# A recommendation tower on one core: the first two blocks of embeddings put in rows by TensorE instead of through memory, and layer 1's weights asked for at another time

## The reference

```python
e = stack([tbl_f[ids[:, f]] for f in range(39)], axis=1)        # 512 x 39 x 16
def cin(X0, Xi, W, b):                                          # W: 128 x (39 * fields of Xi)
    return einsum('hjk,bjd,bkd->bhd', W.reshape(H, 39, -1), X0, Xi) + b[None, :, None]
X1 = cin(e, e, W0, b0)          # 39 x 39 products
X2 = cin(e, X1, W1, b1)         # 39 x 128
X3 = cin(e, X2, W2, b2)
z = concatenate([X1.sum(2), X2.sum(2), X3.sum(2)], axis=1)      # 512 x 384
h = relu(concatenate([z, dense_ctx], 1) @ W_top1 + b_top1)
h = relu(h @ W_top2 + b_top2)
y = h @ W_top3
```

## Time and profile before

| | us |
|---|---|
| median of 3 runs | 669.59 |
| lowest and highest | 668.69, 670.15 |
| the profiled execution's own time | 670.7 |
| its span in the trace | 668.9 |
| TensorE busy | 644.9 (96%) |
| GpSimd busy | 497.0 (74%) |
| ScalarE busy | 480.0 (72%) |
| VectorE busy | 458.9 (69%) |

### The profile page before, as it was taken

One profiled execution on the slowest core, in us unless ns is written; L12 is line 12 of the kernel. 1 busy time (PEld: TensorE's weight loads), 2 busy tenths in 40 slices (PEclk: granted clock), 3 DMA queues, 4 the chain that ended last, 5 costly groups with the idle time before them and its releaser, 6 DMA issues.

```text
span 668.9 us, 11234 instructions
## 1 busy us (share of the span) xinstructions
PE 644.9 (96%) x2676; PEld 479.0 (72%) x2676; DVE 458.9 (69%) x1183; ACT 480.0 (72%) x1737; POOL 497.0 (74%) x467
## 2 busy tenths in 40 slices
PE   3599999999999999999999999999999999999998
PEld 1387677777777777777787777777776777779773
DVE  1367777778686968777725786868687877774920
ACT  1457678878787879697815787878796978784912
POOL 5779888979797988888835797979888886553710
PEclk9989999999999999999999999999999999999999
DMA  6643515151514233251500514132241404002000
GB/s 159 140 100 80 124 26 118 36 120 13 128 27 102 54 75 79 44 111 34 119 11 2 119 13 108 25 81 51 46 85 28 103 10 118 4 4 93 2 0 1
DMA packets 68264, 43.32 MB, mean 65 GB/s; under 512 B 49483, under 2 KB 61710, under 8 KB 66458
## 3 DMA queue, kind: packets, MB, share of 16 engines
q1 hardware_dynamic: 56870, 38.04, 25.4%
q0 software_dynamic: 5184, 1.29, 2.3%
q10 hardware_dynamic: 6158, 3.45, 2.0%
HBM read 39.58 MB, written 1.96 MB: 62 GB/s over the span
## 4 chain that ended last, share of the span: by engine, by line
PE 94%; issue 2%; DVE 1%; DMA 1%; ACT 1%; ACTq 0%; POOLq 0%; POOL 0%; DVEq 0%
PE a_ps L704 40%; PE d_ps L704 25%; PE quad_ps L655 14%; PE quad_ps L758 5%; PE g_ps L745 5%; PE g_ps L814 1%; DMA g_sb<-w_dram 1%; PE quad_ps L672 1%; PE a_ps L871 1%; PE quad_ps L659 1%; PE d_ps L842 1%; ACT parts L930 0%; DVE parts L551 0%; DVE x2t L563 0%; PE a_ps L842 0%
## 5 line engine op out<-in xcount | busy, mean ns | idle before, releaser
L930 ACT ACTIVATE parts<-a_ps,xt 128x128 f32<-128x128 f32 x1536 | 424.1, 383 | 129.7 <-PE a_ps L704 115.3
L551 DVE SCALAR_TENSOR_TENSOR parts<-d_ps,xt,parts 128x128 f32<-128x128 f32 x704 | 201.7, 343 | 108.9 <-PE d_ps L704 98.9
L311 POOL TENSOR_TENSOR parts<-parts 128x512 f32<-128x512 f32 x128 | 163.5, 1293 | 99.3 <-ACT parts L930 98.0
L704 PE MATMUL a_ps<-w_hi,x_hi 128*128 128x512 f32 x384 | 181.3, 472 | 1.5 <-issue 1.5
L311 POOL TENSOR_TENSOR left<-parts 128x512 f32<-128x512 f32 x128 | 167.3, 1323 | 7.5 <-ACT parts L930 5.9
L285 POOL DMA_INDIRECT emb<-tables_dram,rows_now x150 | 144.0, 960 | 25.3 <-issue 18.5
L704 PE MATMUL a_ps<-w_hi,x_lo 128*128 128x512 f32 x384 | 152.4, 397 | 0.6 <-issue 0.6
L704 PE MATMUL a_ps<-w_lo,x_hi 128*128 128x512 f32 x384 | 151.4, 394 | 0.0
L704 PE MATMUL d_ps<-w_hi,x_hi 128*128 128x512 f32 (+1 forms) x256 | 127.0, 496 | 0.9 <-DVE parts L551 0.9
L655 PE MATMUL quad_ps<-products,w_sb 117*128 117x512 f32 (+1 forms) x210 | 107.4, 592 | 0.0
L704 PE MATMUL d_ps<-w_lo,x_hi 128*128 128x512 f32 (+1 forms) x256 | 97.8, 382 | 0.6 <-ACT xt L908 0.6
(11 more groups left out here) (72 smaller groups left out, 428.4 us busy)
## 6 DMA issues: line engine op xcount, KB each, us to landing
shifted<-x_rows SPq DMA_DIRECT2D x45, 312.0 KB
shifted<-x_rows SPq DMA_DIRECT2D x45, 234.0 KB
diag<-xt SPq DMA_DIRECT2D x240, 4.9 KB
rows<-x_rows SPq DMA_DIRECT2D x45, 78.0 KB
emb<-tables_dram,rows_now POOLq DMA_INDIRECT x150
w_sb<-w_dram SPq DMA_DIRECT2D x6, 384.0 KB
shifted<-x_first SPq DMA_DIRECT2D x12, 136.5 KB
g_sb<-w_dram ACTq DMA_DIRECT2D x2, 768.0 KB
```

What stands on the lines that cost most here:

```text
L311: nc.gpsimd.tensor_tensor(to, parts[:, i % 2, now:now + GF, :], parts[:, i % 2, more:more + GF, :], ALU.add).then_inc(pool_added, 1)
L551: nc.vector.scalar_tensor_tensor(now, d_ps[d % D_RING][:, H * at:H * (at + 1)], xt[:, u, i, j:j + 1], before, ALU.mult, ALU.add).then_inc( ...
L704: return nc.tensor.matmul(bank[:, 0:H * len(fields)], x[:, u, 128 * i:128 * (i + 1)], w[:, fields[0]:fields[-1] + 1, :].rearrange("p j h - ...
L930: last = nc.scalar.activation(parts[:, i % 2, 2 + GF * a + at, :], a_ps[(NA * i + a) % A_RING][:, H * at:H * (at + 1)], ACT.Copy, scale=xt ...
```

## The change

Blocks 0 and 1 of the first chunk no longer go through memory. Their gathered rows stand as (8 samples, 16 fields) by 16 elements over the partitions. VectorE spreads each row to eight copies of which all but its own sample's are zero (`spread_first`, a product with a table of ones, `spots`). TensorE sums this with a table of ones (`picker`) into the 39 fields as rows, three times over (`sum_rows`, three float32 matmuls); ScalarE copies this to `rows3` (`copy_first`); TensorE multiplies it with seven tables of ones (`turns`), which gives the seven rotated tiles in PSUM (`turn_rows`, seven float32 matmuls of 39 rows and 128 columns); and VectorE multiplies these with `rows3` (`multiply_turned`). The PSUM banks used are free at that time. `turn_rows(1)` stands behind group 0 of block 0.

The tables come with the small inputs on SP's queue: `masks` is 128 rows of 1468 bytes in place of `mask` (128 of 32 bytes), `turns` is 39 rows of 3276 bytes in place of `ident` (39 of 156 bytes). SP writes and loads only blocks 2 and 3. ScalarE issues the second and the third part of layer 1's weights together, once block 0's gathers have landed; before, the second part was issued at the start and the third after block 0's loads had landed. In VectorE's list `diag_first(0)` now stands ahead of block 1's products and of `split_w1(2)`.

```diff
+TURNED = 2
+TURN_AT = (0, 0)
+        turned_rows = [rows_ps[0:PK, 0:128], g_ps[0:PK, 0:128]]
+        turned_tiles = [(a_ps[0][0:PK, :], a_ps[1][0:PK, 128:512]), (g_ps[0:PK, :], quad_ps[0:PK, 128:512])]
 # SP
-            sp.dma_start(ident[:, :], ident_in).then_inc(small_loaded, 16)
-            sp.dma_start(mask[:, :], mask_in).then_inc(small_loaded, 16)
+            sp.dma_start(masks[:, :], mask_in).then_inc(small_loaded, 16)
+            sp.dma_start(turns[:, :, :], turns_in).then_inc(small_loaded, 16)
-            for i in range(BLKS):
+            for i in range(TURNED, BLKS):
                 write_first(i)
                 load_first(i)
 # VectorE
+            def spread_first(i):
+                dve.wait_ge(first_gathered[i], 16 * GATHERS0)
+                for g0, g1, parts in ((0, GATHERS0 - 1, 128), (GATHERS0 - 1, GATHERS0, LAST_G0)):
...
+                    last = nc.vector.tensor_tensor(to, rows, at, ALU.mult)
+                last.then_inc(spread_ready, 1)
+            def multiply_turned(i):
+                cols = slice(128 * i, 128 * (i + 1))
+                for half, (t0, t1) in enumerate(((0, FIRST_TILES), (FIRST_TILES, QT))):
+                    dve.wait_ge(turned, 2 * i + half + 1)
...
+                    last = nc.vector.tensor_tensor(products[0:PK, t0:t1, cols], tiles, rows, ALU.mult)
+                last.then_inc(first_products, 1)
...
+            spread_first(0)
             split_w1(0)
-            multiply_first(0)
+            multiply_turned(0)
             split_w1(1)
+            spread_first(1)
             low_first(0)
-            multiply_first(1)
+            diag_first(0)
+            multiply_turned(1)
             split_w1(2)
-            diag_first(0)
             first_body()
 # TensorE
+            def sum_rows(i):
+                pe.wait_ge(spread_ready, i + 1)
+                for g in range(GATHERS0):
+                    parts = 128 if g < GATHERS0 - 1 else LAST_G0
+                    mm = nc.tensor.matmul(turned_rows[i], picker[0:parts, g, :], spread[0:parts, i, g, :],
+                                          start=(g == 0), stop=(g == GATHERS0 - 1))
+                mm.then_inc(rows_turned, 1)
+            def turn_rows(i):
+                pe.wait_ge(first_rows, i + 1)
+                for half, (t0, t1) in enumerate(((0, FIRST_TILES), (FIRST_TILES, QT))):
+                    for t in range(t0, t1):
+                        mm = nc.tensor.matmul(turned_tiles[i][half][:, 128 * (t - t0):128 * (t - t0 + 1)], turns[:, t, :],
+                                              rows3[0:FIELDS, 128 * i:128 * (i + 1)], start=True, stop=True)
+                    mm.then_inc(turned, 1)
...
             pe.wait_ge(small_loaded, 64)
+            sum_rows(0)
+            turn_rows(0)
             transpose_first(0)
             pe.wait_ge(w0_ready, 1)
             layer0_first(0)
+            sum_rows(1)
 # ScalarE
+            def copy_first(i):
+                act.wait_ge(rows_turned, i + 1)
+                nc.scalar.copy(rows3[:, 128 * i:128 * (i + 1)], turned_rows[i]).then_inc(first_rows, 1)
...
             load_w1(0)
-            load_w1(1)
             act.wait_ge(small_loaded, 64)
...
             split_w1(0)
-            act.wait_ge(first_written[0], 48)
...
+            act.wait_ge(first_gathered[0], 16 * GATHERS0)
+            load_w1(1)
+            load_w1(2)
+            copy_first(0)
             split_w1(1)
-            act.wait_ge(first_loaded[0], 32 * SPT)
-            load_w1(2)
             store_xt_first(0)
             act.wait_ge(bias_ready, 1)
             high_first(0)
+            copy_first(1)
             split_w1(2)
             first_body()
```

More of the change, by code:

```diff
@@ L146, in build @@
 def build(nc, picks0, picks, tables, x_first, x_rows, w0a, w0b, w1, w2, biases, b1_row, ctx_in, wt1, wt1c, bt1, wt2, bt2, wt3,
-          ident_in, mask_in, out):
+          turns_in, mask_in, out):
     with ExitStack() as stack:
@@ L179, in build @@
         wt3_sb = sb("wt3_sb", [128, N2 // 128])
-        ident = sb("ident", [FIELDS, FIELDS])
-        mask = sb("mask", [128, BLK_B])
+        turns = sb("turns", [FIELDS, QT, PK])
+        ident = turns[:, 0, 0:FIELDS]
+        masks = sb("masks", [128, 2 * BLK_B + GATHERS0 * PK])
+        mask, spots = masks[:, 0:BLK_B], masks[:, BLK_B:2 * BLK_B]
+        picker = masks[:, 2 * BLK_B:].rearrange("p (g k) -> p g k", k=PK)
+        spread = sb("spread", [128, TURNED, GATHERS0, 128])
         shifted = sb("shifted", [128, QT, CW])
@@ L370, in load_first @@
                     sp.dma_start(shifted[rows, :, cols], src).then_inc(first_loaded[i], 16)
[L371 to L373 removed]
+                    src = bass.AP(x_first.tensor, i * X_ROWS0 * 128, [[128, FIELDS], [1, 128]])
+                    sp.dma_start(rows3[rows, cols], src).then_inc(first_loaded[i], 16)
             def write_x(m, half):
@@ L495, in multiply_l0 @@
                                         ).then_inc(products_ready, 1)
+            def spread_first(i):
+                dve.wait_ge(first_gathered[i], 16 * GATHERS0)
+                for g0, g1, parts in ((0, GATHERS0 - 1, 128), (GATHERS0 - 1, GATHERS0, LAST_G0)):
+                    shape = [parts, g1 - g0, BLK_B, D]
+                    to = spread[0:parts, i, g0:g1, :].rearrange("p g (b d) -> p g b d", d=D)
+                    rows = emb0[0:parts, i, g0:g1, :].unsqueeze(2).to_broadcast(shape)
+                    at = spots[0:parts, :].unsqueeze(1).unsqueeze(3).to_broadcast(shape)
+                    last = nc.vector.tensor_tensor(to, rows, at, ALU.mult)
[4 more added lines that the diff above has]
+                    dve.wait_ge(turned, 2 * i + half + 1)
+                    tiles = turned_tiles[i][half].rearrange("p (t c) -> p t c", c=128)
+                    rows = rows3[:, cols].unsqueeze(1).to_broadcast([PK, t1 - t0, 128])
+                    last = nc.vector.tensor_tensor(products[0:PK, t0:t1, cols], tiles, rows, ALU.mult)
+                last.then_inc(first_products, 1)
             def multiply_first(i):
@@ L775, in first_body @@
                             layer0(1, SECOND_L0_AT[i, g])
+                        if (i, g) == TURN_AT:
+                            turn_rows(1)
                         for ahead in FIRST_TRANSPOSE_AT.get((i, g), ()):
@@ L1079 @@
     mask = (np.arange(128)[:, None] // D == np.arange(BLK_B)[None, :]).astype(np.float32)
+    spots = (np.arange(128)[:, None] % BLK_B == np.arange(BLK_B)[None, :]).astype(np.float32)
+    field = FPG0 * np.arange(GATHERS0)[None, :, None] + np.arange(128)[:, None, None] // BLK_B
+    picker = (field == np.arange(PK)[None, None, :] % FIELDS).astype(np.float32).reshape(128, GATHERS0 * PK)
+    turns = (np.arange(FIELDS)[:, None, None] == k.transpose(2, 0, 1).reshape(QT, PK)).astype(np.float32)
     arrays = {
@@ L1089 @@
         "bt2": a["b_top2"].reshape(N2 // 128, 128).T, "wt3": a["W_top3"].reshape(N2 // 128, 128).T,
-        "ident_in": np.eye(FIELDS, dtype=np.float32), "mask_in": mask,
+        "turns_in": turns, "mask_in": np.concatenate([mask, spots, picker], axis=1),
     }
```

10 lines of the change are left out of this document (3 added, 7 removed).

## The result

| us | median | lowest, highest | executions |
|---|---|---|---|
| kernel before | 669.56 | 668.39, 670.61 | 8 |
| changed kernel | 672.18 | 670.28, 675.55 | 8 |

The account below looks back on a forecast made before the run. TensorE alone was taken to bound the body. Hole and half clock -6.9, later group 0 +2.6, turn_rows(1) +1.56: about 2.8 us gained, 666.8 us against 669.59; 8-in-10 range 664.4 to 669.8.

Parts of the forecast that it names:

- The start: TensorE's first 45 us: warm-up 1.1 us later from the tables, group 0 2.6 later, group 7 2.8 us earlier.
- no hole up to group 7: Sign in the trace: TensorE has no hole over 0.5 us between group 0 and group 7 of block 0.
- The 1.0 us ahead of x1_hi: Unexplained gap between block 0's layer 0 end and ScalarE's x1_hi, kept as a bound of 0 to 1.0 us.
- the chain starts at the warm-up's end: Block 0's new steps wait for the warm-up, not the gathers, so most of the saved memory time can't be had.
- Everything ahead of it changes, everything behind it has the same lists: Costing at block 0's group 7: its start, 39.62 before and 36.84 forecast, was taken to carry the gain.
- VectorE's products for blocks 2 and 3 come from memory as before, but SP no longer works on blocks 0 and 1 first, so they are earlier, not later: Check for waits between group 0 and group 7: these products' loads were expected earlier than before, with no size given.
- a second hole: Sign of a wrong forecast: second TensorE idle stretch behind group 0, blamed on the weights' third part or VectorE's order.
- given back later: GpSimd's additions near 80 us hold VectorE up; price 1.5 to 2.8 us, 669.2 us; chance 0.16 with late third part.
- the slower rival: TensorE's clock halves in the start's small matmuls: 669.6 to 674.1, about 671.9 us; chance 0.12 with a like stall.
- the sparse stretch: TensorE from 21.8 to 28.4 us, small matmuls with 4.5 us of work in 6.6, where the clock might fall.
- The rule that the prediction took from the Trainium skill: Clock gated by TensorE's recent busyness, throttled by default; a copy or spread late by some us would halve it.
- a like stall: Unspecified stall counted with the falling clock as the slower outcome, together chance 0.12.

Follow-up runs that it names:

- e4: Changed kernel with 4 warm-up matmuls in place of 8: 667.2 us, ratio 0.9972 to the kernel before.
- g4: The changed kernel as it stands, measured again on another chip: 678.5 us, ratio 1.0132 to the kernel before.
- j4: Changed kernel with SyncE's writes and loads of blocks 2 and 3 held until block 0's layer 0 is done: 677.8 us, ratio 1.0129.
- k1: Changed kernel with layer 1's weights asked for at the old time, as in the kernel before: 671.35 us, ratio 1.0030.
- j3: Changed kernel with GpSimd's ten gathers for chunk 1 held until block 1's layer 0 is done: 680.9 us, ratio 1.0181.
- e1: Changed kernel with the products of blocks 2 and 3 two places earlier in VectorE's list: 679.8 us, ratio 1.0057.
- f1: Changed kernel with ScalarE copying the rows of blocks 2 and 3 to PSUM as one operand of VectorE's product: 673.6 us, ratio 1.0028.
- f2: Changed kernel with its three new tables laid behind all other buffers in SBUF: 680.4 us, ratio 1.0134.
- g1: Changed kernel with the new tables behind all other buffers and 4 warm-up repeats: 671.15 us, ratio 1.0007.
- g3: Changed kernel with the new tables behind all other buffers and 2 warm-up repeats: 668.95 us, ratio 0.9984.
- e2: Changed kernel with three of GpSimd's gathers moved from behind its four additions to between them: 682.6 us, ratio 1.0167.
- f0: The changed kernel as it stands, measured again: 680.4 us, ratio 1.0148 to the kernel before.
- g2: Changed kernel with 3 extra TensorE products behind block 0's transpose and 2 behind its layer 0: 678.7 us, ratio 1.0066.
- j1: Changed kernel with shift tables and their rows rounded to float32r, one matmul instruction per product instead of two: 679.2 us, ratio 1.0100.
- j2: Kernel before with 6 warm-up repeats in place of 8 and short float32 matmuls added at block 0: 669.6 us, ratio 0.9993.
- k2: Kernel before with parts 1 and 2 of layer 1's weights asked for once block 0 is gathered: 668.8 us, ratio 0.9987.
- e3: Kernel before with only diag_first(0) moved ahead of block 1's products and the weight split in VectorE's list: 670.1 us, ratio 1.0000.
- f3: Kernel before with 4 warm-up repeats in place of 8: 669.75 us, ratio 1.0007.

## Why the prediction was wrong, point by point

**The start, right.** Warm-up at 11.90 (forecast 12.6, bounds 11.5 to 13.0), 9.55 long; layer 0 at 25.17 (25.25); group 0 at 28.30 (28.4); no hole up to group 7, at 37.16 (36.84). The gain there was 2.46 us of the 2.8. That layer 0 came within 0.1 us of the forecast is luck in part: the tables delayed the warm-up by 0.37 us and not by 1.1, and the chain behind it was 0.6 longer than added up (the warm-up 9.55 for 9.35, sum_rows(0) 1.00 for 0.67). From group 0 to group 7 it took 8.86 us for 8.44. The 1.0 us ahead of x1_hi, kept as a bound, did not come (0.11). That the chain starts at the warm-up's end was right too, and undoing it (`e4`) gave 4.2 us there.

**The step that failed** is "Everything ahead of it changes, everything behind it has the same lists", and with it "VectorE's products for blocks 2 and 3 come from memory as before, but SP no longer works on blocks 0 and 1 first, so they are earlier, not later". The lists behind group 7 are the same, but the engines do not move together: GpSimd is bound by its gathers and stays where it was (its additions start at 38.21, and at 37.71 in the kernel before), VectorE moves by 2.55 us, and their order at one pair of instructions turns round. The step had the wait for the loads and not the wait for the other engine: the product was taken at its 1.09 us wherever it fell. It took 5.44 us in the profiled execution, 5.33 in `g4`, 5.31 in `j4`, 5.42 in `k1`; 1.08 where it met no addition (`j3`, `e4`, `e1`). The hole of 3.04 to 3.06 us alone takes back the whole gain. That a run without the hole is faster by as much is not shown: `e1` and `f1` have other delays in many executions, and their full-clock ones, 0.6 under the kernel before and level with it, are 2.2 and 1.6 us better than the changed kernel's (1.6 over), not 3. The full-clock executions of the changed kernel and of `k1` spread from 669.5 to 672.7 us, and the two profiled ones among them (`g4`, `k1`), which have the whole hole, are at 672.5, so that others may have met a shorter wait. I had looked for a second hole only up to group 7, and the rival "given back later" looked 40 us too late, at 80 us.

**The clock** fell, as the slower rival said, but not in the sparse stretch: behind the hole. There it cost 2.8 us (2.85 forecast) in the first profiled execution; `j4`'s had it too, while those of `g4` and `k1` had the same hole and the full clock. The rule that the prediction took from the Trainium skill (TensorE: Matmul & The Clock Gate, "Part 1: The HAM clock gate"), by which the danger lies in waits, agrees with two of the four. That the slower rival's case, 671.9 us, lies near the measured 672.2 is chance: it was made of half clock ahead of group 7, and at full clock the kernel took 671.2.

**The loop**, costed at nothing by the same sentence, is slower by 0.25 us in three chunks, 1.2 to 1.4 in all. It is the place of the buffers in SBUF (`f2`, `g1`, `g3`: rate of before with the new tables laid behind the others). Which buffer is read more slowly there was not tried.

**At full clock and without late starts** the sum is: -2.6 at group 7, +3.0 hole, +1.3 loop, +0.1 at the joints = +1.8 (`k1`: spans 670.7 and 668.9).

**The long executions** (late starts of 1 to 7 us between 24 and 40 us in their profiles) are the largest part where they occur, 5 to 12 us. In the experiments 40 of 62 executions of versions with 8 repeats and the sooner weights took over 676 us (`e1`, `e2`, `f0` to `f2`, `g2`, `g4`, `j1`, `j4`; `j3` and the one of 833 us not counted), two of `g1`'s twelve with 4 repeats, and none of the kernel before or of its four variants; the eight of the result had none. The runs speak against each of these as the one cause: the number of short matmuls (`j1`, `j2`), TensorE having nothing behind them (`g2`), the transfers of blocks 2 and 3 from 21 us on (`j4`, which only puts them off to 27 us), the sooner weights alone (`k2`). Open: what makes TensorE's completions late, in both kernels, and whether turning and weights together do.

**Chances.** Slower had 0.12, for the clock or a like stall; the lock was not among the cases.

## What to carry to other kernels

A change that moves one engine and not another changes which of two instructions comes first, so look in the trace, well past the changed place, for VectorE instructions with two SBUF operands that will now start behind a GpSimd addition. If a warm-up ends after its successor's data are there, try a shorter one with the change, and look at the clock behind it (`e4` gained 0.3%; `g1` had the full clock in two of twelve executions). Put new tables behind the buffers that the loop reads, and compare the loop's period, not only the start.

## What was not expected of the hardware

VectorE's product, met by four GpSimd additions in a row, waited for all four when it began in the first of them (4.4 us for a 1.08 us instruction, four profiles), and only for the one in progress when it began in the second or third (0.2 to 0.9 us, `e3`, `f3`, `j2`, `g1`). The same loop ran 0.2% slower with its buffers 7.6 kB further up in SBUF (7816 bytes of tables a partition in place of 188). And VectorE and ScalarE can start 1 to 7 us after the last matmul that they wait for has ended by the trace, in the changed kernel's family and, without long executions, in variants of the kernel before.
